# One of six depthwise units of a convolution chain computed on GpSimd instead of VectorE

## The reference

```python
def _L2_conv_ref(x, Wr, br, Wpw, bpw, Wdw, bdw, Wpwl, bpwl, ...):
    rw = jax.nn.sigmoid(jnp.mean(x, axis=(1, 2)) @ Wr + br)          # 4 routing weights per image
    h = einsum('bhwc,bcm->bhwm', x, einsum('be,ecm->bcm', rw, Wpw)) + (rw @ bpw)   # 48 -> 192 channels
    h = relu(_bn(h, g1, b1, m1, v1))
    h = _cond_dw(h, Wdw, bdw, rw)                                     # depthwise 3x3, weights mixed by rw
    h = relu(_bn(h, g2, b2, m2, v2))
    h = einsum('bhwm,bmf->bhwf', h, einsum('be,emf->bmf', rw, Wpwl)) + (rw @ bpwl)  # 192 -> 48 channels
    return _bn(h, g3, b3, m3, v3) + shortcut
```

## Time and profile before

| | before |
|---|---|
| median of 3 runs | 1163.04 us (1160.52 to 1165.03) |
| the profiled execution | 1161.86 us, its span 1160.0 us |
| TensorE busy | 1049.4 us (90% of the span) |
| VectorE busy | 858.6 us (74%) |
| ScalarE busy | 470.9 us (41%) |
| GpSimd busy | 90.4 us (8%) |

### The profile page before, as it was taken

One profiled execution on the slowest core, in us unless ns is written; L12 is line 12 of the kernel. 1 busy time (PEld: TensorE's weight loads), 2 busy tenths in 40 slices (PEclk: granted clock), 3 DMA queues, 4 the chain that ended last, 5 costly groups with the idle time before them and its releaser, 6 DMA issues.

```text
span 1160.0 us, 14937 instructions
## 1 busy us (share of the span) xinstructions
PE 1049.4 (90%) x4808; PEld 667.8 (58%) x4808; DVE 858.6 (74%) x1193; ACT 470.9 (41%) x812; POOL 90.4 (8%) x72
## 2 busy tenths in 40 slices
PE   4699789998999999999999999999999999977986
PEld 3465566556665666556665666557565666535534
DVE  6742569976798669976899659976799669972870
ACT  3311533354533643354533633354523643334331
POOL 0300011000200011000200011000200011000000
PEclk9889979999999999999999989999999999989998
DMA  4224325236423545236523535236423551236114
GB/s 67 60 53 73 73 39 88 48 77 127 91 32 72 112 85 87 45 76 125 101 33 80 109 73 87 45 72 124 94 34 79 111 87 43 47 71 131 21 24 97
DMA packets 169904, 86.79 MB, mean 75 GB/s; under 512 B 145455, under 2 KB 146324, under 8 KB 169876
## 3 DMA queue, kind: packets, MB, share of 16 engines
q1 hardware_dynamic: 169876, 86.44, 40.1%
HBM read 10.82 MB, written 6.29 MB: 15 GB/s over the span
## 4 chain that ended last, share of the span: by engine, by line
PE 63%; DVE 13%; issue 9%; SPq 6%; ACT 4%; DMA 4%; POOL 0%; DVEq 0%; ACTq 0%; POOLq 0%
PE bank L1132 12%; PE bank L1137 12%; PE bank L1143 8%; DVE dwa L659 6%; PE bank L1166 5%; PE bank L1113 4%; PE bank L1234 4%; DMA x_odd<-y_parts 3%; PE bank L1154 3%; PE bank L1181 3%; SPq L903 2%; PE bank L1182 2%; PE bank L1105 2%; SPq L876 2%; PE bank L1169 2%
## 5 line engine op out<-in xcount | busy, mean ns | idle before, releaser
L659 DVE SCALAR_TENSOR_TENSOR dwa<-h1a,dyn,dwa 128x1024 f32<-128x1024 f32 x240 | 293.2, 1276 | 0.0
L659 DVE SCALAR_TENSOR_TENSOR dwb<-h1b,dyn,dwb 128x1024 f32<-128x1024 f32 x128 | 155.9, 1275 | 0.0
L1132 PE MATMUL bank<-y_parts,w_l 96*96 96x512 f32 x576 | 152.1, 409 | 0.0
L1137 PE MATMUL bank<-y_parts,w_h 128*96 128x512 f32 x576 | 148.7, 402 | 0.0
L1166 PE MATMUL bank<-a_parts,wt_h 128*112 128x512 f32 x384 | 118.2, 416 | 11.8 <-ACT dwa L1448 7.7
L1132 PEld LDWEIGHTS bank<-y_parts,w_l 96*96 96x96 f32 x576 | 91.7, 163 | 61.0 <-issue 21.3
L1137 PEld LDWEIGHTS bank<-y_parts,w_h 128*96 128x96 f32 x576 | 93.8, 163 | 44.6
L1166 PEld LDWEIGHTS bank<-a_parts,wt_h 128*112 128x112 f32 x384 | 64.1, 177 | 46.0 <-issue 16.9
L1003 POOL TENSOR_TENSOR y_parts<-y,y_parts 96x512 fp32r<-96x512 f32 x56 | 67.1, 1199 | 203.6 <-DVE y L699 203.5
L1398 ACT ACTIVATE y<-bank,b2s 96x512 f32<-96x512 f32 x32 | 21.9, 683 | 141.2 <-PE bank L1143 141.2
L1143 PE MATMUL bank<-y_parts,w_one 128*96 128x512 f32 x192 | 76.6, 399 | 0.0
(11 more groups left out here) (246 smaller groups left out, 1706.9 us busy)
## 6 DMA issues: line engine op xcount, KB each, us to landing
y_parts<-a_parts SPq DMA_DIRECT2D x64, 198.0 KB, 3.0
y_parts<-a_parts SPq DMA_DIRECT2D x64, 197.6 KB, 3.4
tok<-in_x_dram SPq DMA_DIRECT2D x48, 192.0 KB, 4.8
a_parts<-a_parts SPq DMA_DIRECT2D x128, 66.0 KB, 2.4
y_parts<-y_parts SPq DMA_DIRECT2D x64, 131.9 KB, 2.3
x_even<-y_parts SPq DMA_DIRECT2D x16, 384.0 KB, 7.5
x_odd<-y_parts SPq DMA_DIRECT2D x16, 384.0 KB, 9.9
out_dram<-dwb SPq DMA_DIRECT2D x32, 192.0 KB, 4.1
```

The source lines that it names most:

```text
L659: nc.vector.scalar_tensor_tensor(out=dst, in0=tap_input(n, t), scalar=weight, in1=dst, op0=ALU.mult, op1=ALU.add).then_inc(tap_step, 1)
L1132: nc.tensor.matmul(bank[0:C2, :], w2_l[:, t, :], y1_h[:, rows, cols], start=t == 0, stop=False)
L1137: nc.tensor.matmul(bank[0:C2, :], w2_h[:, t, :], y1_parts[:, 0, rows, cols], start=False, stop=False)
```

## The change

Unit 1 (the lower half of `dwb`) is made by GpSimd. It has no fused multiply-add with a scalar here, so each tap is a product into a spare buffer and an addition, and each of these covers 8 rows, 512 elements (the buffer's size): 9 taps x 2 halves x 2 = 36 instructions of 128x512 for an image. Each waits by semaphore for the one ahead of it. The spare buffer is the third `y1` buffer, widened from 112 to 128 partitions. The weight is read through a broadcast view (`everywhere`). For image i the unit stands in GpSimd's queue behind `split_y1(i + 1)` and ahead of `scale_k(i + 2)`, which is the stage of conv2.

VectorE keeps units 0, 2, 3, 4 and 5, that is 41 steps, in the order: taps of 0 and 2 in turn, taps of 3 and 4 in turn, taps of 5 alone. `steps_at` becomes (6, 4, 4, 4, 4, 3, 4, 4) and (1, 1, 3, 3). ScalarE finishes units 0 and 2 at k = 5, unit 1 at k = 6 (a wait for GpSimd's 18th addition), unit 3 at k = 7, units 4 and 5 as before.

```diff
-        y1_buffers = sb("y1", [P2, Y1_BUFFERS, BANK])
+        y1_buffers = sb("y1", [128, Y1_BUFFERS, BANK])
...
+        POOL_UNIT, POOL_TAPS = 1, 2 * TAPS
+        pool_product = y1_buffers[:, Y1_BUFFERS - 1, :].rearrange("p (j w) -> p j w", w=W)
+
+        def in_turn(*units):
+            return [(n, t) for t in range(TAPS) for n in units if t > 0 or n < OTHER_UNITS]
+
+        STEPS = in_turn(0, 2) + in_turn(3, 4) + in_turn(5)
+        LAST_STEPS = in_turn(0, 1) + in_turn(4, 5)
+        TAP_STEPS = len(STEPS)
...
-        steps_at = (0,) * CHUNKS + (7, 4, 4, 4, 4, 4, 4, 4) + (1, 1, 6, 7)
+        steps_at = (0,) * CHUNKS + (6, 4, 4, 4, 4, 3, 4, 4) + (1, 1, 3, 3)
...
                     else:
-                        dve.wait_ge(tap_step, TAP_STEPS * image + s - 1 - skipped)
+                        if (n, t - 1) in order:
+                            dve.wait_ge(tap_step, TAP_STEPS * image + order.index((n, t - 1)) + 1)
...
+            def unit_taps(image, y1_images):
+
+                _, dst, c, _ = unit(POOL_UNIT)
+                pool.wait_ge(y1l_ready, POOL_CHUNKS * y1_images)
+                after(pool, stored, 16 * STORES * image)
+                pool.wait_ge(h1b_ready, H1B_WRITES * (image + 1))
+                def everywhere(at):
+                    return columns(dyn[:, :], at, [[0, ROWS], [0, W]])
+
+                for t in range(TAPS):
+                    for half in range(2):
+                        rows, done = slice(half * ROWS, (half + 1) * ROWS), 2 * t + half
+                        if done > 0:
+                            pool.wait_ge(pool_tap, POOL_TAPS * image + done)
+                        nc.gpsimd.tensor_tensor(pool_product, tap_input(POOL_UNIT, t)[:, rows, :], everywhere(Y_DW + c * TAPS + t),
+                                                ALU.mult).then_inc(pool_times, 1)
+                        pool.wait_ge(pool_times, POOL_TAPS * image + done + 1)
+                        sum_so_far = dst[:, rows, :] if t > 0 else everywhere(Y_DWB + c)
+                        nc.gpsimd.tensor_tensor(dst[:, rows, :], sum_so_far, pool_product, ALU.add).then_inc(pool_tap, 1)
+
             scale_k(0)
             split_y1(0)
-            with pool.Fori(1, IMAGES) as image:
+            scale_k(1)
+            split_y1(1)
+            unit_taps(0, 2)
+            scale_k(2)
+            split_y1(2)
+            with pool.Fori(3, IMAGES) as image:
+                unit_taps(image - 2, image)
                 scale_k(image)
                 split_y1(image)
+            unit_taps(IMAGES - 2, IMAGES)
...
-            def finish_unit(image, n, skipped=0):
+            def finish_unit(image, n, order=STEPS):
                 _, dst, _, _ = unit(n)
-                act.wait_ge(tap_step, TAP_STEPS * image + last_step(n) - skipped)
+                if n == POOL_UNIT and order is STEPS:
+                    act.wait_ge(pool_tap, POOL_TAPS * (image + 1))
+                else:
+                    act.wait_ge(tap_step, TAP_STEPS * image + last_step(n, order))
                 nc.scalar.activation(dst, dst, ACT.Relu).then_inc(h2_ready, 1)
...
-                        for n in finished_at(BY_CONV2 + k):
+                        for n in {5: (0, 2), 6: (1,), 7: (3,)}.get(k, ()):
                             finish_unit(back, n)
```

More of the change, by code:

```diff
@@ L183, in conv_chain_kernel @@
         xq = sb("xq", [C2 + 1, 2, BANK])
-        y1_buffers = sb("y1", [P2, Y1_BUFFERS, BANK])
-        y1, x2_m = y1_buffers[0:C2, :, :], y1_buffers[:, 0:2, :]
+        y1_buffers = sb("y1", [128, Y1_BUFFERS, BANK])
+        y1, x2_m = y1_buffers[0:C2, :, :], y1_buffers[0:P2, 0:2, :]
         y1_parts = sb("y1_parts", [128, 2, H + 2, WP], F32R)
@@ L269, in conv_chain_kernel @@
         project_weight_chain = Chain(sem("project_weight_chain"), 4)
-        tap_step = sem("tap_step")
+        tap_step, pool_tap, pool_times = sem("tap_step"), sem("pool_tap"), sem("pool_times")
         A_XT, A_QK, A_G, A_M2, A_XQ = 0, 4, 12, 13, 14
@@ L298, in conv_chain_kernel @@
         UNITS = OTHER_UNITS + H // UNIT_ROWS
-        FIRST_STEPS, PAIR_STEPS = 2 * TAPS, 2 * (TAPS - 1)
-        TAP_STEPS = FIRST_STEPS + (UNITS - 2) // 2 * PAIR_STEPS
+        POOL_UNIT, POOL_TAPS = 1, 2 * TAPS
[5 more added lines that the diff above has]
+        TAP_STEPS = len(STEPS)
         BY_CONV1, BY_CONV2, BY_PROJECT = 0, CHUNKS, 2 * CHUNKS
-        steps_at = (0,) * CHUNKS + (7, 4, 4, 4, 4, 4, 4, 4) + (1, 1, 6, 7)
+        steps_at = (0,) * CHUNKS + (6, 4, 4, 4, 4, 3, 4, 4) + (1, 1, 3, 3)
         assert sum(steps_at) == TAP_STEPS
@@ L318, in tap_input, with last_step @@
             return src[:, r0 + t // 3:r0 + t // 3 + UNIT_ROWS, t % 3:t % 3 + W]
[L320 to L333, removed]
+        def last_step(n, order=STEPS):
+            return order.index((n, TAPS - 1)) + 1
         PE_UNITS = (2, 3)
@@ L639, in depthwise_at, with depthwise @@
                     chosen = range(done, done + steps_at[place])[steps]
[L640 to L645, removed]
+                    depthwise(image, STEPS, chosen, 1)
+            def depthwise(image, order, chosen, first_of_act):
+                for s in chosen:
+                    n, t = order[s]
                     _, dst, c, _ = unit(n)
@@ L652, in depthwise @@
                     if n >= 2 and t == 1:
-                        dve.wait_ge(tap1_ready, (UNITS - 2) * image + n - 1 - (len(PE_UNITS) if skipped else 0))
+                        dve.wait_ge(tap1_ready, (UNITS - 2) * image + n - first_of_act)
                     if t == 0:
@@ L825, in iteration @@
                 if attn is None:
-                    depthwise(f, 0, FIRST_STEPS)
-                    depthwise(f, FIRST_STEPS + PAIR_STEPS, TAP_STEPS, skipped=PAIR_STEPS)
+                    depthwise(f, LAST_STEPS, range(len(LAST_STEPS)), 1 + len(PE_UNITS))
             prepare_conv2()
@@ L1535, in _ @@
             for n in range(OTHER_UNITS):
-                finish_unit(IMAGES - 1, n)
+                finish_unit(IMAGES - 1, n, LAST_STEPS)
             for n, b in enumerate(PE_BANKS):
@@ L1541, in _ @@
             for n in range(OTHER_UNITS + len(PE_UNITS), UNITS):
-                finish_unit(IMAGES - 1, n, skipped=PAIR_STEPS)
+                finish_unit(IMAGES - 1, n, LAST_STEPS)
             for m in range(PCHUNKS):
```

## The result

| | before | after |
|---|---|---|
| median of 3 runs | 1163.04 us | 1369.95 us (1351.05 to 1389.39) |
| ratio to before, 95% interval | | 1.1695 [1.1551, 1.184] |
| profiled execution, its span | 1161.86, 1160.0 | 1389.39, 1387.6 |
| steady iteration | 129.0 us | 163.7 us (673.0 to 836.7) |

The change makes the kernel 17% slower.

A forecast was written before the change was run, and what follows sets the result against it. TensorE was taken to bound the kernel beside conv2, VectorE following with no room. Span: 1160.0 + 238.7 (L1 later) - 11.1 (waits gained) + 21 (clock) = 1408.6 us, so about 1411 us, 21% slower; range 1270 to 1490.

The forecast's parts named there:

- the 23.0 us of waits: TensorE's 14 waits for ScalarE's relu of a depthwise unit, the most that removing VectorE steps could give back.
- Steps and instructions exclude each other, in both directions: Beside conv2, a VectorE step and a GpSimd instruction, both reading two SBUF inputs, block each other; chance 0.70.
- The sum to T, 81.0 us: 37.8 us of VectorE work and 43.2 us of GpSimd instructions beside conv2, one after the other.
- T: The moment GpSimd's unit 1 is ready, forecast at 521.8 us, some 36 us after ScalarE could take it.
- The low bound, a hold of 0.80 us: GpSimd holds VectorE off only for the size-dependent part of each instruction; with no clock fall, 1289 us in all.
- The chain behind T, 10.2 us: From unit 1 ready through relu, l1 parts, three steps, y2, w3 and projection 1 to the start of L1.
- The gain of 11.1 us: What remains of the relu waits without the first projection's, gained over the span because unit 5 is ready early.
- The clock, 21 us: After TensorE's idle time the granted clock falls, two 4 us stretches an iteration at about 1.5 us each.
- clock stays low: Rival: TensorE gets the low clock through conv2 and into l1, 10 to 15 us more an iteration, about 1490; chance 0.06.
- Who waits: In conv2 TensorE works at VectorE's pace, idle nearly 4 of 10 us; ScalarE waits some 35 us for GpSimd.
- No contention: Rival: steps and GpSimd instructions pass each other; about 1145 us with short waits, 1183 with the full 0.24; chance 0.09.
- One direction only: Rival: GpSimd keeps VectorE off but is not kept off itself; 1183 to 1293 us, middle 1240; chance 0.15.

The follow-up runs named there:

- run 11: Kernel before, no GpSimd unit, VectorE's 50 steps reordered so units 0 to 3 end earlier, units 4 and 5 still in turn: 1146.65 us, ratio 0.9875.
- run 10: Kernel before, no GpSimd unit, VectorE's 50 steps reordered for both relu waits, unit 4 also ahead of unit 5: 1154.47 us, ratio 0.9937.
- run 1: Kernel before plus 36 GpSimd products of two SBUF tiles beside conv2, which nobody waits for: 1325.38 us, ratio 1.1369.
- run 2: Kernel before plus 72 GpSimd memsets of 128x512 beside conv2, which only write: 1162.48 us, ratio 0.999.
- run 4: Changed kernel with VectorE's steps behind the first tap replaced by one-input sums for images 0 to 6, part of the computation left out: 1136.55 us, ratio 0.9788.
- Run 3: Kernel before plus 36 GpSimd products by a constant beside conv2, each reading one SBUF tile, which nobody waits for: 1257.83 us, ratio 1.0851.
- run 7: The changed kernel again, unaltered: 1343.99 (the profiled one), 1343.71, 1387.5 and 1632.57 us.
- run 9: Changed kernel with 104 filler matmuls on TensorE ahead of the first projection: 1358.49 us, ratio 1.1684.

## Why the prediction was right, and where it was off

**What bounds the kernel.** Right, with one reserve: the 23.0 us of waits are not all to be had. Removing the first projection's gives what it shows and a little more (run 11); removing the third's too gave less in all (run 10).

**Steps and instructions exclude each other, in both directions.** Right. It was argued from 1.03 against 0.19 us at one small instruction; shown by runs 1, 2 and 4: load that reads 1.1369, load that only writes 0.999, VectorE on one input 0.9788. The reserve is in run 4: the first tap has one tile as input and was held all the same. The direction that had no row before has one in `after` (products at 1.90 us beside steps, 1.04 alone). The rule of the Trainium skill (SBUF — State Buffer, "Who interferes with whom") agrees with all three, the steps undisturbed by writes and the undisturbed sums included. Where the page says ("SBUF: two separate sides") that the other one is blocked for the whole instruction, the trace says somewhat less, below. Run 3 adds that a one-input GpSimd instruction is mostly the one that waits.

**The sum to T, 81.0 us.** Right in kind, 4.9 us too long. Its VectorE part had the right instructions: up to the wait at place 7 there are one L700, one L651, 29 steps at L656 and two L735. Alone, GpSimd's 36 come to 18 x 1.04 + 18 x 1.26 = 41.4 us, where the step said 43.2, and the waits between them leave 0.07 us, 35 x 0.07 = 2.5 us. So one after the other would be 37.8 + 41.4 + 2.5 = 81.7. The part that failed is "one after the other": a round costs VectorE 1.98 - 1.21 = 0.77 us beside a product and 2.24 - 1.21 = 1.03 beside an addition, 0.3 less than the 1.11 and 1.33 that these take alone with their gap. Of the 36 instructions 18 took 1.9 to 2.2 us in this way, 18 x 0.32 = 5.8 us, and 81.7 - 5.8 = 75.9 against 76.1 measured. The low bound, a hold of 0.80 us, was the better value for products and too low for additions. Waiting steps showed 2.06 and 2.31 us, near the 2.4 that the prediction named.

**The chain behind T, 10.2 us.** It is 10.3 us in run 7, where the clock came back, and 13.3 in the profile of after, where it did not until l1. L1 was forecast 91.2 us into the iteration and came at 86.6 and 89.6.

**The gain of 11.1 us.** Nearly right in run 7, not in the profile of after. In run 7 the part behind L1's start is 70.8 us against 71.9 in before, 1.1 us an iteration of the 1.6 forecast; on average of six iterations it is 71.2 against 72.8. In the profile of after it is 74.1 in every one: the third projection's wait is gone, and the clock stood at 0.67 from 812 to 820. Run 10 shows such a fall without any GpSimd unit, and so does before, though not in the iteration that was looked at: its clock was at 0.58 from 678 to 686, and at 0.57 in the earlier trace rows. What it hangs on is open.

**The clock, 21 us.** Right on the middle only. It is about zero in run 7 and about 7 x 6.3 = 44 us in the profile of after; the two executions differ by 45 us. The rival "clock stays low" was priced at 1490; of the seven executions of this kernel one took 1632.57 us at 0.602. No profile shows where its clock was low, so that rival is neither shown nor excluded by it.

**Who waits.** Partly wrong. The prediction had TensorE at VectorE's pace in conv2, idle for nearly 4 of 10 us. It was busy for 46.08 of 50 us, and conv2 ended 7 us late (729.7 less 673.0, 56.7 in place of 49.5). Of the first 50 us 3.9 are idle (0.65 in before), and a clock of 0.93 in place of 1.00 costs some 3.5 us of them, as an estimate. It was no more because at times GpSimd stood back instead: from 703 to 721 it got two instructions through, and its last 12 ran alone, behind 734. The total does not change by that, since whoever stands back is served later; but the loss shows at the projection, 146.2 us in 7 waits of 20.9 us, and not inside conv2. ScalarE waited 181.3 / 7 = 25.9 us for GpSimd, not 35.

**The rivals.** "No contention" needed T under 489.3 us, that is 48.5 us for the unit; run 4 met it with 45.9 us and gained 2%. Its price of about 1145 us was a wrong sum: 36 x (1.199 + 0.06) = 45.3 us make T 486.1, and 7 x 3.2 = 22 us less than 1163 is 1141. Run 4 measured 1136.55. "One direction only" is excluded by the rounds.

Sum of the differences: T 7 x 4.9 = 34 us less than forecast gives 1377 us, and the median is 1370. That this is so near is in part luck: the clock's term, forecast at 21 us, is anything from zero to 44.

## What to carry to other kernels

Before work goes to an idle engine, count the inputs in SBUF on both sides: two on each meant that their times add (less 0.3 us a round), one on GpSimd that GpSimd waits, and "idle beside conv2" was no free room here, though GpSimd's busy row said 0.00 and writes alone would have cost the steps nothing. The count is not all of it: the first tap, with one tile, was held too (1.52 us in place of 0.81), so look at each instruction's own row in a short trial. No run tried another way to do a tap on GpSimd than a product and an addition. A single odd row (1.03 us where its twin takes 0.19) was enough to see it coming. Then look at which of the waits the change is after can be had by order alone: here a new order took half of them and gave 1.2%, and removing the rest brought a wait for a transfer and a lower clock instead.

## What the runs showed of the hardware that was not expected

- **Turns are not fair.** GpSimd's instruction mostly gets every other turn, but at times none for 13.15 us (in the profile of after once in each of 7 iterations, 12.75 to 13.15 us), up to 21.96 us in run 1 and 23.30 in run 3, while VectorE's steps follow each other. The waits of 12 to 13 us ended where VectorE read PSUM twice in a row (714.15 to 715.47), and not at the single read at 708.71; it is so in all seven iterations. The 5.15 us one ended at a single read, and so did waits of 14.85 and 8.14 us in run 1. No experiment was made on that, and the rule stays open.
- **A hold is shorter than the instruction**: 0.77 us of 1.11, 1.03 of 1.33.
- **Writes leave the steps alone, and not every instruction with one tile is left alone.** Beside 504 memsets with a median of 0.525 us the steps stayed at 1.273 us, ratio 0.999. The first tap, `tensor_scalar` on one tile, took 0.998 us beside memsets and 1.518 beside products and additions, 0.809 alone.
- **The unit is steady, the clock behind it is not**: 76.1 us in both profiles, and then, in the 12 us behind it, 0.50, 0.64 and 1.00 in one and 0.50 throughout in the other. What decides between the two is open.
- **A short wait behind a busy stretch can be followed by the low level too**: 2.00 us idle, then 0.58 (run 9); behind 1.40 us it stayed at 1.00 in the iteration ahead. These are two iterations of one profile, and no more than that.
